# Spreading the preparation and the finishing of batches over an iteration, in an attention and expert kernel

## What is computed

```python
# 1. cross attention: 16 heads of 32, one key and one value head for all of them
xn = layernorm(x)
Q, K, V = xn @ Wq + bq, ctx @ Wk + bk, ctx @ Wv + bv
x1 = x + softmax(Q @ K.T * 32 ** -0.5) @ V @ Wo + bo
# 2. delta-rule memory, 4 heads of 128, on the normalised x1 (chunks of 64 tokens)
xn2 = layernorm(x1)
rk = xn2 / norm(xn2)                       # per head
o = memory(v=xn2 @ Ww.T, rk, decay)        # needs the inverse of a unit triangular matrix
x2 = x1 + xn2 + alpha * o @ Wr.T
# 3. mixture of experts: each token goes to its best of 16 experts, 128 places per expert
xn3 = layernorm(x2)
gate = softmax(xn3 @ Wg)
out = x2 + gate_max * relu(xn3 @ w1[e]) @ w2[e]
```

## Time and profile before

| | us |
|---|---|
| time, median of 3 runs | 2423.58 (2422.32 to 2427.81) |
| the profiled execution, its own time | 2427.98 |
| its span, first to last instruction | 2426.1 |
| mean granted TensorE clock, share of full speed | 0.946 |

### The profile page before, as it was taken

The page is one execution under the profiler, slowest core; times in us unless marked ns, Lnnn a source line. Parts: engine busy times, 40 slices in busy tenths (PEclk is TensorE's granted clock), DMA queues, the critical chain, the costliest instruction groups (busy, mean ns, idle before and its releaser), DMA issues. The chain is left out here.

```text
span 2426.1 us, 35019 instructions
## 1 busy us (share of the span) xinstructions
PE 2189.4 (90%) x12608; PEld 1429.9 (59%) x12608; DVE 1371.0 (57%) x2311; ACT 1193.3 (49%) x2237; POOL 1638.2 (68%) x1323
## 2 busy tenths in 40 slices
PE   5889898989998989898989898989898769999999
PEld 3435555546464646464646464645554448999998
DVE  2665757566667566666666666666665433333333
ACT  3555554646464646464645455555554313333333
POOL 0676878677777777777777777777777714655655
PEclk9889998999899989998999899989998889999999
DMA  4532120202020202121211111121120009999995
GB/s 160 188 113 66 40 82 24 83 23 83 23 83 23 83 26 80 40 66 40 66 47 58 51 59 63 43 66 42 59 79 9 18 14 375 350 363 346 362 363 189
DMA packets 108157, 263.75 MB, mean 109 GB/s; under 512 B 9849, under 2 KB 35065, under 8 KB 99792
## 3 DMA queue, kind: packets, MB, share of 16 engines
q1 hardware_dynamic: 98448, 235.32, 27.7%
q10 hardware_dynamic: 5952, 14.29, 1.6%
q0 software_dynamic: 3584, 11.90, 1.2%
HBM read 223.74 MB, written 25.72 MB: 103 GB/s over the span
## 5 line engine op out<-in xcount | busy, mean ns | idle before, releaser
L917 POOL TENSOR_TENSOR psum<-psum,p 128x512 f32<-128x512 f32 x896 | 1162.9, 1298 | 291.7 <-ACT p L553 197.7
L708 DVE TENSOR_REDUCE mpart<-bank 128x1 f32<-128x512 f32 x1024 | 675.0, 682 | 403.5 <-PE bank L357 396.1
L553 ACT ACTIVATE p<-bank 128x512 f32<-128x512 f32 x1024 | 596.8, 600 | 553.5 <-PE bank L370 543.6
L357 PE MATMUL bank<-kT,qT 96*128 96x512 f32 x1024 | 484.1, 480 | 62.6 <-DVE mpart L708 32.5
L370 PE MATMUL bank<-qT,kT 97*128 97x512 f32 x1024 | 502.4, 492 | 4.7 <-ACT p L553 4.0
L357 PEld LDWEIGHTS bank<-kT,qT 96*128 96x128 f32 x1024 | 199.6, 196 | 211.5 <-DVE mpart L708 104.6
L370 PEld LDWEIGHTS bank<-qT,kT 97*128 97x128 f32 x1024 | 201.7, 197 | 142.6 <-issue 113.6
L382 PE MATMUL bank<-p,v 128*32 128x512 f32 x2048 | 271.4, 651 | 0.0
L1159 POOL TENSOR_TENSOR w2l<-w,w2h 128x1024 fp32r<-128x1024 f32 x64 | 203.2, 3177 | 75.1 <-PE ebank L1074 54.4
L332 PE MATMUL bank<-cst,w_first 128*128 128x128 f32 x1024 | 164.1, 287 | 21.7 <-DMA w_first<-in_ctx 18.0
L332 PEld LDWEIGHTS bank<-cst,w_first 128*128 128x128 f32 x1024 | 134.3, 149 | 64.9 <-issue 29.4
(11 more groups left out here) (159 smaller groups left out, 3137.8 us busy)
## 6 DMA issues: line engine op xcount, KB each, us to landing
w<-in_w SPq DMA_DIRECT2D x48, 2048.0 KB, 20.1
w_first<-in_ctx SPq DMA_DIRECT2D x64, 1024.0 KB, 4.9
w_first<-in_w SPq DMA_DIRECT2D x16, 2048.0 KB, 11.6
dispatched<-route ACTq DMA_DIRECT2D x17, 513.0 KB, 4.4
dis<-dispatched SPq DMA_DIRECT2D x16, 513.0 KB, 3.5
qT<-qh SPq DMA_DIRECT2D x128, 64.0 KB, 2.0
xin<-in_x SPq DMA_DIRECT2D x16, 256.0 KB, 2.6
qT<-qs SPq DMA_DIRECT2D x64, 64.0 KB, 2.0
```

What stands on the lines that cost most here:

```text
L357: e.matmul(a[:], qT[b % 2][0:3 * HD, (4 * g + h) * P:(4 * g + h + 1) * P], kT[b % 2][0:3 * HD, c * 512:(c + 1) * 512], start=True, stop=Tr ...
L553: e.activation(p[n % NP][:], B_BANK[u % 2][:], ACT.Exp).then_inc(p_act.sem, 1)
L708: e.tensor_reduce(mpart[g % 2][:, n:n + 1], A_BANK[(17 * g + n) % 2][:], AX.X, ALU.max).then_inc(max_dve.sem, 1)
L917: e.tensor_tensor(acc[:], first[:], p[(UNITS * b + u) % NP][:], ALU.add).then_inc(psum_pool.sem, 1)
```

## The change

The tables are rewritten, and the loops pass a tick of more than one iteration to `prepare` and `finish`, so that a batch's preparation may begin in the iteration before (negative ticks) and its finishing end in the one after (ticks over 127).

- Context tiles stand 6 ticks apart, at ticks -19 to 71, where they stood 4 apart at 8 to 68; K/V chunks at 4, 28, 52, 76 instead of 23, 39, 55, 71.
- x is normalised and the query products are done an iteration ahead, the products at ticks 82, 86, 90, 94 of the iteration before (-46 and so on); the queries are sent at tick 2 instead of 38, after a new wait for the last score of two batches before.
- Finishing starts later: `xb` at 8 instead of 2, `sums` at 17 instead of 9, and all that follows with it; the routing (`xn3` to `row`) falls at ticks 130 to 143, that is 2 to 15 of the next iteration. Each product of `x1`, `V` and `x2` has two ticks to the next instead of one.
- `sums(b)` waits for the first K/V chunk of batch b+2 instead of the last of batch b+1; the waits of the other users of `KV_BANK` follow the new order.
- The semaphores `post_*` are split into `post_*` (up to IT) and `late_*` (from Vn), since parts of two batches' finishing now interleave. There is one iteration more at the front, and a tail of 16 ticks at the end.

The core of the diff (the other engines' loops change as the last one shown; where a step only waits on `late_*` instead of `post_*` it is left out):

```diff
 TICKS = 2 * UNITS
 GROUP = 2 * KB
-NORM, XN, XNT, QPROJ, QSEND = 1, 5, 10, 27, 38
-TILE_AT = [8 + 4 * k for k in range(KB)]
-KV_AT = [TILE_AT[4 * c + 3] + 3 for c in range(4)]
-VT_AT = [KV_AT[2 * m + 1] + 7 for m in range(2)]
-LOAD_AT = [t + 6 for t in TILE_AT[3::4]]
-POST = dict(xb=2, sums=9, recip=[9, 10, 11, 12], att=13, x1=15, x1_add=18, norm2=19, xn2=22, ss=23, x12=24, rn=24,
-            xn2T=25, rk=27, V=28, V_copy=31, rkT=34, I=38, XT1=40, X1=44, Vn=98, oT2=101, x2=104, x2_add=107,
-            store=108, norm3=108, xn3=111, xn3T=115, lg=118, eg=119, oh=120, loc=123, row=125)
-LEVEL_AT = [[47 + 9 * n, 50 + 9 * n, 53 + 9 * n] for n in range(LEVELS)]
+
+NORM, XN, XNT, QPROJ, QSEND = -62, -58, -51, [-46, -42, -38, -34], 2
+TILE_AT = [6 * k - 19 for k in range(KB)]
+KV_AT = [TILE_AT[4 * c + 3] + 5 for c in range(4)]
+VT_AT = [38, 82]
+LOAD_AT = [t + 4 for t in TILE_AT[3::4]]
+
+POST = dict(xb=8, sums=17, recip=[18, 20, 21, 23], att=24, x1=[26, 28, 30, 32], x1_add=33, norm2=34, xn2=36, ss=37,
+            x12=38, rn=39, xn2T=39, rk=41, V=[42, 44, 46, 48], V_copy=49, rkT=51, I=54, XT1=57, X1=60, Vn=114,
+            oT2=117, x2=[120, 122, 124, 126], x2_add=127, store=129, norm3=128, xn3=130, xn3T=133, lg=136, eg=137,
+            oh=138, loc=141, row=143)
+LEVEL_AT = [[63 + 9 * n, 66 + 9 * n, 69 + 9 * n] for n in range(LEVELS)]
+TAIL = POST["row"] + 1 - TICKS
...
             def send_queries(b):
 
+                if b >= 2:
+                    e.wait_ge(*b_pe.at(b - 2, UNITS - 1))
                 for part, src, ready in ((0, qh, q_act), (1, qh, q_act), (2, qs, q_pool)):
...
-            for i in range(-1, B + 1):
-                for t in range(TICKS):
-                    if t == XNT + 2 and i + 2 < B:
-                        load_x(i + 2)
-                    if t == QSEND and i + 1 < B:
+            for i in range(-2, B + 2):
+                for t in range(TICKS if i <= B else TAIL):
+                    if t == XNT + 2 + TICKS and i + 3 < B:
+                        load_x(i + 3)
+                    if t == QSEND and 0 <= i + 1 < B:
                         send_queries(i + 1)
...
                 if b:
-                    e.wait_ge(*post_dve.at(b - 1, "before"))
-                if b + 1 < B:
-                    e.wait_ge(*kvs_dve.at(b + 1, 3))
+                    e.wait_ge(*late_dve.at(b - 1, "before"))
+                if b + 2 < B:
+                    e.wait_ge(*kvs_dve.at(b + 2, 0))
                 for out, lhs, src in ((KV_BANK, cst[:, C_ONES, 0:HD], psum), (P_BANK, cst[:, C_STACK, 0:HD], oS)):
...
-                    if c:
-                        e.wait_ge(*kvs_dve.at(b, c - 1))
-                    elif b:
-                        e.wait_ge(*(o_dve.at(b - 2, "recip3") if b > 1 else kvs_dve.at(0, 3)))
-                    if c == 1:
-                        e.wait_ge(*q_dve.at(b))
+                    e.wait_ge(*(kvs_dve.at(b, c - 1) if c else q_dve.at(b)))
+                    if c == 1 and b >= 2:
+                        e.wait_ge(*o_dve.at(b - 2, "recip3"))
...
-                if POST["x1"] <= t < POST["x1"] + DC:
-                    ins = project(P_BANK, turned, wo, t - POST["x1"])
-                    if t == POST["x1"] + DC - 1:
+                if t in POST["x1"]:
+                    ins = project(P_BANK, turned, wo, POST["x1"].index(t))
+                    if t == POST["x1"][3]:
                         ins.then_inc(post_pe.sem, 1)
...
-            for i in range(-1, B + 1):
+            for i in range(-2, B + 2):
                 if i == 1:
                     e.wait_ge(*w_in.at(WEIGHTS - 1))
                     e.wait_ge(*zeroed.at(ZEROES - 1))
-                for t in range(TICKS):
+                for t in range(TICKS if i <= B else TAIL):
                     if 0 <= i < B and t % 2:
                         add_weights(i, t // 2)
-                    if i + 1 < B:
+                    if 0 <= i + 1 < B:
                         prepare(i + 1, t)
-                    if i >= 1:
+                    if i + 2 < B:
+                        prepare(i + 2, t - TICKS)
+                    if i >= 2:
+                        finish(i - 2, t + TICKS)
+                    if 1 <= i <= B:
                         finish(i - 1, t)
```

More of the change, by code:

```diff
@@ L190, in attention @@
         o_dve = named("o_dve", "recip0 recip1 recip2 recip3 att")
[L193 to L197, removed]
+        post_pe = named("post_pe", "x1 xn2T V rkT I X1")
+        post_act = named("post_act", "ss0 ss1 ss2 ss3 xn2T rk0 rk1 rk2 rk3 V rkT X1")
+        post_dve = named("post_dve", "x1 st2 mv2 xn2 XT1a MT IT")
+        post_pool = named("post_pool", "xb ve2 rs2 x12 rm rn MT0 XT0 XT1")
+        late_pe = named("late_pe", "Vn oT2 x2 xn3T lg loc")
+        late_act = named("late_act", "Vn oT2 xn3T eg")
+        late_dve = named("late_dve", "x2 st3 mv3 xn3 lg0 lmax emax cand best oh ohloc before loc valid locc row0 row "
+                         "d0 d1 sidx gate token token1")
+        late_pool = named("late_pool", "ve3 rs3")
         y_pe, z_pe, xt_pe = count("y_pe", LEVELS), count("z_pe", LEVELS), count("xt_pe", LEVELS - 1)
@@ L311, in _ @@
                         e.dma_start(xr[:], T["x"][i - 1]).then_inc(xr_in.sem, 16)
-                    if t == POST["store"] and i >= 1:
-                        e.wait_ge(*post_dve.at(i - 1, "x2"))
-                        e.dma_start(T["out"][i - 1], x2).then_inc(x2_out.sem, 16)
+                    for b, at in ((i - 2, t + TICKS), (i - 1, t)):
+                        if at == POST["store"] and 0 <= b < B:
+                            e.wait_ge(*late_dve.at(b, "x2"))
+                            e.dma_start(T["out"][b], x2).then_inc(x2_out.sem, 16)
                     if t == LOAD_AT[3] and i == LAST - 1:
```

224 lines of the change are left out of this document (115 added, 109 removed).

## The result

| | before | after |
|---|---|---|
| time, us, median of 4 runs each | 2425.7 (2422.3 to 2428.5) | 2510.4 (2509.5 to 2512.4) |
| ratio, 95% interval | | 1.035 (1.033 to 1.037) |
| span of the profiled execution, us | 2426.1 | 2508.1 |
| mean granted clock of TensorE | 0.946 | 0.926 |

The account below looks back on a forecast made before the run. TensorE, busy 90% of the span, was taken as the bound. Thirteen intervals of +5.0 us give +65; with -2, +2 and +8 the span goes from 2426.1 to 2499.1, the time to 2497 us, range 2415 to 2545.

Parts of the forecast that it names:

- The added wait: GpSimd's first add of group 0 waits for the moved sums, 15 adds queue ahead of norm2; sums to xn2's transposes 26.1 us.
- B: TensorE's stretch from the sums to the transposes of xn2: from a mean of 20.1 us to 26.1 (25 to 27).
- A: TensorE's stretch from the last product of x2 to the end of the sums: from 22.5 us to 20.6.
- C: TensorE's stretch from xn2's transposes to those for X1: from 22.15 us to 20.8, including 2.0 for late rk.
- D: TensorE's stretch from the transposes for X1 to the next last product of x2: from 53.0 us to 55.3.
- Start: Kernel start: batch 1's queries and four tiles run before the first score, mostly under VectorE's maxima; +2 us (0 to 6).
- The DMA queue. Cost 0: The queries' twelve transfers move from tick 38 to 2 at no cost; the first pass's later chunk is inside the +2.
- First interval and end: First interval after batch 0: -2 us; kernel end, last sums queued behind batch 14's routing on TensorE: +8 (0 to 14).
- Rival 1: Spreading pays if GpSimd's backlog isn't the latest at xn2's transposes and rk: interval 116.1, about 2400 us; chance 0.16.
- Clock stays full when spread: Rival 1's further form: TensorE's clock also holds 2.4 GHz, 5 us less each time, 2345 us.
- rival 2: Costs and gains cancel across the interval, gains elsewhere being up to 4 us larger than counted: 2410 to 2435 us; chance 0.06.
- rival 3: VectorE is the bound in A and B; A 25 us, interval 127, 2555 us; chance 0.06.

Follow-up runs that it names:

- e1: The changed kernel with a second accumulator for group 0 of odd batches and 17 instead of 18 buffers of exponentials: 2489.6 us, ratio 1.026.
- e8: e1 with the four query products back at ticks 34 to 40 of their own iteration, queries sent at 48: 2450.8 us, ratio 1.011.
- e9: Kernel before with only the change's tile and K/V ticks, x normalised an iteration ahead, queries at 20 to 23, old finishing: 2397.9 us, ratio 0.990.
- e4: The change's whole preparation (tiles every 6 ticks, queries an iteration ahead) with the finishing at the ticks of the kernel before: 2476.3 us, ratio 1.021.
- e11: e5 with the whole preparation (x, queries, tiles) 4 ticks later: 2369.6 us, ratio 0.978.
- e7: The changed kernel plus 32 unused transposes of the identity on TensorE ahead of the wait for xn2: 2513.3 us, ratio 1.036.
- e6: Only the change's finishing ticks, preparation at the ticks of the kernel before, one accumulator and 18 buffers: 2439.5 us, ratio 1.006.
- e5: e6 with a second accumulator for group 0 and 17 buffers: 2453.5 us, ratio 1.011.

## Why the prediction was right, and where it wasn't

The forecast was 2497 with 2415 to 2545; measured 2510.4. The added wait that it named is there. That the interval came out as forecast is in part luck: the 5.0 us that it added were work and waiting alone, and of the 5.0 us measured 3.0 are a lower clock, which it expected unchanged. By its steps:

- **The added wait: right.** GpSimd is idle 16.9 us (said 14 to 18), then come 15 adds in a row, and its rsqrt isn't idle for VectorE. The transposes of xn2 wait 5.6 us, a little over the 3 to 5 that were said. B is 26.4 (said 26.1, 25 to 27). The 15 adds took 20.9 us (4.06 + 5.45 + 11.42 in the rows, start to start), said 21.0. rk waits 1.10 us for rn, as said. e1 shows the wait to be the cause of B's length: 26.4 to 22.1.
- **The stretches.** A 20.3 (said 20.6), C 21.8 (20.8), D 54.3 (55.3), interval 122.7 (122.8). The errors of C and D cancel. Of C's 21.8 us, 1.9 are waiting (2.0 were said) and 2.4 the clock (nothing was said); and C is 21.8 in e1 too, where the backlog is gone. The oh step did fall to 0.23 us.
- **Start: mis-sized.** Said +2 (0 to 6), measured 4.2 + 8.6 = +12.8. This term failed, and with it "The DMA queue. Cost 0", which put the first pass inside the 2. In that pass the twelve transfers of the queries are issued at 71 to 80 us, beside the loads of the weights; those of `qs` then take 8.3 us to land (2.7 before), and the context chunks 11.4 in the median (5.8). A row of maxima issued at 96.56 reached TensorE only at 107.13, the 6.59 us wait above. In all later iterations together such waits are 0.6 us. The waits for these rows up to the first exponential of batch 1, in after and then in e8, where the queries' transfers are issued at 107 to 115 us:

```profile
PE bank L387 <- DMA qT<-mrow: 8.8, 2, 6.6
...
PE bank L392 <- DMA qT<-mrow: 5.1, 3, 2.5
```

So the late rows don't come from the queries' transfers alone. e8 starts the scores of batch 1 at 166.3 us where e1 starts them at 178.3: 12.0 us go with the queries that are prepared ahead, and 8.3 of them lie before the first exponential (66.6 and 74.9).
- **First interval and end.** -3.8 (said -2) and +8.5 (said +8, from 8.3 of idle routing; the waits are 7.3). The steady part is +64.5 (said +65). The sum of spans is short by 10.8 - 1.8 - 0.5 + 0.5 = 9.0 us. The other 4.4 us of the miss are the step from span to time: it took off 4.4 us, since before's profiled execution stood that far above its median, and after's stands 0.5 below its own.
- **The clock: wrong.** "I expect as much low clock as before": it was 9.9 us an interval and is 17.7. That is 3.0 of the 5.0 us. The stretches were sized right all the same, since other terms were too large. D shows it over the first ten intervals: it grew by 1.5 us, of which the clock is +1.7 (3.4 us low, none before), the waiting -1.2 (2.1 to 0.9), and the added work only +1.0, where 2.3 were said. So it is luck that the missing term and the terms that were too large cancel.
- **Rival 1, what would be without the backlog: wrong.** It gave 20.6 + 21.4 + 18.8 + 55.3 = 116.1 and 2400 us; e1 is that kernel and has 23.3 + 22.1 + 21.8 + 54.4 = 121.6 and 2490. A of 20.6 held only while GpSimd stands idle, so the backlog gave back in A a part of what it took in B: the prediction counted the saving in both cases. C of 18.8 was TensorE's own work, and that was even less (21.8 less 3.8 of waiting less 0.2 for the clock is 17.8), but the waits were left out. e9, which has the products of V one tick apart and not two, does C in 18.5; that this distance makes the waits is argued, no run changes it alone. So the direction was right with a cause whose removal gives back 0.9 of the 3.5 points; 2.1 points are there with the spread preparation alone (e4).
- **"Clock stays full when spread" (rival 1's further form).** Neither so for the whole change, nor wrong as an idea: e9 and e11 have 3.4 us of low clock.
- **Sums of the rivals.** Three don't come out as written: 5 us less in each of 13 intervals from 2400 is 2335 and not 2345; rival 2's 4 us give 2497 - 52 = 2445 and not 2410 to 2435; rival 3's terms add up to 2557.5. The forecast doesn't rest on them.

What the rows say of the clock: in after it fell behind waits of 1 to 2 us in A and B and of 5.64 us ahead of xn2, and was still low in C behind the latter (0.89). The Trainium skill, page TensorE: Matmul & The Clock Gate, section "HAM oscillation — how this bites in real kernels", describes such kernels: TensorE waits, the clock drops, and the work behind starts slow, in each turn of the loop. The trace agrees for after and before. The section's remedy is to arrange the loop so that TensorE stays at the full clock. e7 filled 3.66 us of the wait with transposes and kept 17.1 us of low clock, so no run here shows a gain from filling a wait; e11, whose waiting is the least (7.3 us), has 3.4 us of low clock, but so has e9 with 11.2 us of waiting.

Open: what decides how long the clock stays low behind a wait. In e9 and e4 the two long waits at the start of B are alike, 1.5 and 2.3 us, 26 and 28 us into the interval, and the low time behind them is 3.4 us in the one and 6.9 in the other, with 3.4 more in C. That the clock is 5.5 of the 6.2 us is shown by the accounts; which move of work makes the clock fall is not shown by anything here. Open too is what makes the rows of maxima late in the first pass beside the queries' transfers.

## What to carry to other kernels

When a schedule in ticks is moved, list for each moved step what the queues of the other engines hold between its old and its new place: one add that waits for a moved sum held up 15 adds, xb, the scatter and the normalisation behind it. Then test each half of the change alone and both together: here one move gained 1% alone, the other changed nothing, and the two together lost 2.1%; late finishing (with two accumulators) lost 1.1%, and with the preparation 4 ticks later as well it gained 2.2%. Where one engine is busy nine tenths of the time, split the interval into its waiting, half its low-clock time while busy and the rest; the rest nearly stays, and the two others say where the time went.

## What the runs showed of the hardware

- Some small steps of VectorE (128x16) depend on GpSimd, in one and the same place of the kernel: the oh step (L854 in after) took 0.23 us beside an idle GpSimd (after and e6) and 0.98 to 1.17 beside a busy one (e1, e5 and before). The reductions beside it took 0.16 to 0.17 us in all of them. An engine held up by a wait can thus speed up its neighbour. A is 15.9 us in e6 and 18.6 in e5, but 1.7 of these 2.7 us are the clock (none low in e6's A, 3.4 us in e5's).
- The granted clock is a term of its own size: 3.4 to 19.5 us low of each interval in kernels with the same work, worth 1.6 to 8.6 us.
- 32 transposes of 128 columns in a wait (3.66 us in the timeline of e7) left the low clock at 17.1 us an interval (17.7 without them) and the time where it was (2513.3 against 2510.4).
- In the first iteration of after a 2 KB transfer reached its reader 10.6 us after its issue (96.56 to 107.13). The queries' transfers had landed by then (the last at 88.7 us); transfers of 513 KB that write `dispatched` (10.6 to 11.4 us each) and a 1 MB chunk (12.4) were under way.
